# First attention of a macaron block: shared values weighed for two heads at once in three rounded passes, outputs one to two steps later

## What is computed

```python
q = (x @ w_q).reshape(bsz, q_len, 32, 128).transpose(0, 2, 1, 3)
k = (x @ w_k).reshape(bsz, q_len, 8, 128).transpose(0, 2, 1, 3)
v = (x @ w_v).reshape(bsz, q_len, 8, 128).transpose(0, 2, 1, 3)
lq = x @ w_lq
lk = (lq @ w_lk).reshape(bsz, q_len, 32, 128).transpose(0, 2, 1, 3)
lv = (x @ w_lv).reshape(bsz, q_len, 32, 128).transpose(0, 2, 1, 3)
...
k = jnp.repeat(k, 4, axis=1)
v = jnp.repeat(v, 4, axis=1)
attn = _causal_attn(q, k, v, SCALE)
lat = _causal_attn(q, lk, lv, SCALE)
...
return attn @ w_o + lat @ w_lo
```

## Time and profile before

| | us |
|---|---|
| median of 3 runs | 1806.8 |
| lowest, highest | 1804.63, 1810.41 |
| profiled execution, whole | 1806.92 |
| its span | 1805.0 |
| PE busy | 1739.7 (96%) |
| VectorE, ScalarE, GpSimd busy | 1098.4, 1084.0, 928.9 |
| granted clock of TensorE, mean | 0.997 of full |

### The profile page before, as it was taken

How to read it: one execution, slowest core, us unless ns; L and a number is a source line. 1 busy time by engine, 2 the same in 40 slices (tenths; PEclk the granted TensorE clock), 3 DMA queues, 4 the chain that set the end, 5 groups by cost and what they waited for, 6 DMA issues and landing times.

```text
span 1805.0 us, 32176 instructions
## 1 busy us (share of the span) xinstructions
PE 1739.7 (96%) x11116; PEld 1518.6 (84%) x11116; DVE 1098.4 (61%) x3305; ACT 1084.0 (60%) x3077; POOL 928.9 (51%) x1170
## 2 busy tenths in 40 slices
PE   7989999999999999999999999999999998899798
PEld 6779989989999998999999899989888776677567
DVE  6665465456456555644654664565565677888756
ACT  3355565566566656755665665576563264888964
POOL 4555544555554555554455555455542255777850
PEclk9999999999999999999999999999999999999999
DMA  4300021012001101200110120011012111000101
GB/s 145 108 22 13 7 71 36 1 36 71 7 17 61 36 1 42 65 7 19 59 36 1 48 65 1 18 60 36 1 54 64 42 52 55 1 2 2 37 12 47
DMA packets 35424, 65.79 MB, mean 36 GB/s; under 512 B 4032, under 2 KB 4672, under 8 KB 35264
## 3 DMA queue, kind: packets, MB, share of 16 engines
q1 hardware_dynamic: 35264, 63.73, 11.5%
HBM read 61.62 MB, written 2.10 MB: 35 GB/s over the span
## 4 chain that ended last, share of the span: by engine, by line
PE 74%; DVE 8%; ACT 8%; issue 6%; POOL 3%; DMA 0%; SPq 0%; DVEq 0%; POOLq 0%; ACTq 0%
PE bank L363 57%; PE bank L1105 6%; PE bank L1092 4%; PE bank L1107 3%; ACT s L1219 2%; PE bank L1677 2%; PE bank L1648 1%; ACT s L1743 1%; DVE h L761 1%; PE bank L1664 1%; DVE work L1324 1%; DVE work L772 1%; POOL h L839 1%; DVE x L1393 1%; ACT h L684 1%
## 5 line engine op out<-in xcount | busy, mean ns | idle before, releaser
L363 PE MATMUL bank<-W,oT 128*128 128x512 f32 x1632 | 432.1, 400 | 0.8 <-DVE x L1880 0.8
L1430 POOL TENSOR_TENSOR qk<-work,qk 128x512 fp32r<-128x512 f32 (+1 forms) x160 | 192.9, 1206 | 431.9 <-ACT qk L1210 431.8
L363 PEld LDWEIGHTS bank<-W,oT 128*128 128x128 f32 x1632 | 288.3, 189 | 48.5 <-DVE x L1880 1.2
L1226 ACT COPY pt<-bank 128x384 f32<-128x384 f32 x256 | 122.0, 476 | 324.1 <-PE bank L1092 323.8
L1422 POOL TENSOR_TENSOR work<-work,table 128x512 f32<-128x512 f32 (+1 forms) x160 | 191.3, 1195 | 134.3 <-ACT work L1205 134.3
L1219 ACT ACTIVATE s<-s,neg_max 128x128 f32<-128x128 f32 (+1 forms) x512 | 227.6, 445 | 49.8 <-DVE neg_max L1338 48.3
L363 PE MATMUL bank<-W,xnA 128*128 128x320 f32 (+1 forms) x1056 | 190.1, 334 | 2.3 <-DVE xnA L348 1.7
L1315 DVE TENSOR_TENSOR work<-bank,table 128x512 f32<-128x512 f32 (+1 forms) x160 | 102.0, 638 | 129.4 <-ACT work L1205 129.4
L363 PEld LDWEIGHTS bank<-W,xnA 128*128 128x128 f32 x1056 | 165.6, 188 | 14.7 <-DVE xnA L348 2.6
L363 PE MATMUL bank<-qk 128*128 128x256 f32 (+1 forms) x768 | 166.0, 351 | 0.9 <-POOL qk L1430 0.9
L1358 DVE COPY lvv<-bank 128x320 f32<-128x320 f32 x128 | 62.9, 491 | 170.1 <-PE bank L363 170.0
(11 more groups left out here) (111 smaller groups left out, 3495.9 us busy)
## 6 DMA issues: line engine op xcount, KB each, us to landing
raw<-in_weights SPq DMA_DIRECT2D x215, 256.0 KB, 2.7
x<-in_x SPq DMA_DIRECT2D x8, 256.0 KB, 5.2
out<-x SPq DMA_DIRECT2D x8, 256.0 KB, 2.1
row<-in_bias_rows SPq DMA_DIRECT2D x5, 256.0 KB, 2.8
table<-in_constants SPq DMA_DIRECT2D x4, 240.0 KB, 3.0
b_qk<-in_bias_rows SPq DMA_DIRECT2D x1, 512.0 KB, 3.7
b_val<-in_bias_rows SPq DMA_DIRECT2D x1, 256.0 KB, 3.1
table<-in_constants SPq DMA_DIRECT2D x1, 66.0 KB, 2.6
```

Of the source, the lines that this page charges most:

```text
L363: last = nc.tensor.matmul(out_ap, lhs(i), rhs(j), start=start and k == 0, stop=stop and k == 2)
L1226: nc.scalar.copy(pt0[:, k, :], bank[PT][:, 0:3 * P]).then_inc(a_pt, 1)
L1430: nc.gpsimd.tensor_tensor(lo, work[:, 2 + s, st.columns(what)], hi.bitcast(F32), ALU.subtract).then_inc(a_rope_lo, 1)
```

## The change

The shared values get a high and a low part of their own, `vs`. The shared probabilities of two heads are kept, in high and low parts, in `pt_pair`; the own probabilities stay in plain float32 (`pt_own`). In every second step (h=0 and h=2) `weigh_pair` multiplies both heads' shared probabilities by the shared values, in three passes of 512 columns and three of 256, and fills the whole bank `OB`. `weigh_own` is the weighing of before, for the own values alone, and stands once in each step. Results go to `o_pair` and `o_own`. The outputs of the shared part come one to two steps after the pair's weighing has its operands: none in h=2, two in h=1, one each in h=3 and h=0. Weight chunk 13 is split in step 3 instead of step 17, chunk 12 in 17 instead of 16, and the waits for chunks follow the new places of the outputs.

`turn(1)` now waits for `a_pt_lo`, the low part of the probabilities that `turn(0)` left in the bank. VectorE makes it (`turned_lo`) right behind the rotation.

```diff
-SPLIT_AT = {2: [17, 14], 3: [18], 11: [1], 12: [0, 2], 13: [3, 6], 14: [4, 7], 15: [8, 9],
-            16: [10, 11, 15, 12], 17: [16, 13]}
+SPLIT_AT = {2: [17, 14], 3: [18, 13], 11: [1], 12: [0, 2], 13: [3, 6], 14: [4, 7], 15: [8, 9],
+            16: [10, 11, 15], 17: [16, 12]}
...
-WEIGHTS_FOR = {2 + h: [C_WO + h, C_WLO + h] for h in range(GH)}
+WEIGHTS_FOR = {2: [C_WLO], 3: [C_WO, C_WLO + 1], 4: [C_WO + 1, C_WLO + 2],
+               5: [C_WO + 2, C_WO + 3, C_WLO + 3]}
...
-                lvv = sb(s, "lvv", [P, 2, LVW])
-                pt0 = sb(s, "pt0", [P, 2, 3 * P])
-                oT0 = [sb(s, f"oT0_{i}", [P, 4, SEQ], F32R) for i in (HI, LO)]
+                lvv = sb(s, "lvv", [P, 2, GH * HD])
+                vs = [sb(s, f"vs{i}", [P, 2, HD], F32R) for i in (HI, LO)]
+                pt_pair = [sb(s, f"pt_pair{i}", [P, 2, 3, P], F32R) for i in (HI, LO)]
+                pt_own = sb(s, "pt_own", [P, 3 * P])
+                o_pair = [sb(s, f"o_pair{i}", [P, 2, SEQ], F32R) for i in (HI, LO)]
+                o_own = [sb(s, f"o_own{i}", [P, 2, SEQ], F32R) for i in (HI, LO)]
...
             def turn(k):
-                n, s = st.near(-1).inst(k)
+                n, s = before.inst(k)
                 pe.wait_ge(a_norm, n + 1)
-                pe.wait_ge(a_pt, n + 1)
+                if k == 0:
+                    pe.wait_ge(a_pt_own, before.number() + 1)
+                else:
+                    pe.wait_ge(a_pt_lo, before.number() + 1)
                 for blk in range(3):
                     last = nc.tensor.transpose(bank[PT][:, blk * P:(blk + 1) * P],
                                                s0[:, s, blk * P:(blk + 1) * P], ident)
                 last.then_inc(a_turned, 1)
...
-            def weigh(k):
-                before = st.near(-1)
-                n, _ = before.inst(k)
-                col = before.h * P if k else GH * P
-                if before.h == 0 and k == 0:
+            def weigh_pair():
+                pe.wait_ge(a_pt_lo, before.number() + 1)
+                pe.wait_ge(a_own_lo, before.number() + 1)
+                to = bank[OB][:, :].rearrange("p (e q) -> p e q", e=2)
+                product(to, lambda p: vs[p][:, 0, :],
+                        lambda p: pt_pair[p][:, :, 0:2, :].rearrange("p e b q -> p e (b q)"), True, False)
+                product(to[:, :, P:SEQ], lambda p: vs[p][:, 1, :],
+                        lambda p: pt_pair[p][:, :, 2, :], False, True).then_inc(a_pv_pair, 1)
+
+            def weigh_own():
+                col = before.h * P
+                if before.h == 0:
                     pe.wait_ge(a_proj_free, before.fill(3)[0] + 3)
-                pe.wait_ge(a_pt, n + 2)
-                pe.wait_ge(a_o_lo, n + 1)
-
-                nc.tensor.matmul(bank[OB][:, 0:SEQ], lvv[:, 0, col:col + P], pt0[:, k, 0:2 * P],
+                pe.wait_ge(a_pt_own, before.number() + 2)
+                if before.paired():
+                    pe.wait_ge(a_pair_lo, before.pair() + 1)
+                else:
+                    pe.wait_ge(a_own_lo, before.number() + 1)
+
+                nc.tensor.matmul(bank[OB][:, 0:SEQ], lvv[:, 0, col:col + P], pt_own[:, 0:2 * P],
                                  start=True, stop=False)
-                nc.tensor.matmul(bank[OB][:, P:SEQ], lvv[:, 1, col:col + P], pt0[:, k, 2 * P:3 * P],
-                                 start=False, stop=True).then_inc(a_pv, 1)
-
-            def output(k):
-                done = st.near(-2)
-                n, s = done.inst(k)
-                first, end = done.h == 0 and k == 0, done.h == GH - 1 and k == 1
+                nc.tensor.matmul(bank[OB][:, P:SEQ], lvv[:, 1, col:col + P], pt_own[:, 2 * P:3 * P],
+                                 start=False, stop=True).then_inc(a_pv_own, 1)
...
+            def output(k, done):
...
+                if k:
+                    pe.wait_ge(a_own_lo, done.number() + 2)
+                    of, slot = o_own, done.number() % 2
+                else:
+                    pe.wait_ge(a_pair_lo, done.pair() + 1)
+                    of, slot = o_pair, done.h % 2
                 w = ((C_WLO if k else C_WO) + done.h) * CH
                 for tt in range(2):
-                    last = product(bank[OUTB[tt]][:, :], lambda p: oT0[p][:, s, tt * P:(tt + 1) * P],
+                    last = product(bank[OUTB[tt]][:, :], lambda p: of[p][:, slot, tt * P:(tt + 1) * P],
...
+            if lag2 and st.h == 0:
+                output(0, st.near(-3))
+            if lag1 and before.paired():
+                weigh_pair()
             if lag1:
-                weigh(0)
                 turn(1)
             if st.queries and not st.first:
                 a0_queries(pe, st)
@@ -1139,12 +1181,16 @@
                 if t == 0:
                     pe.wait_ge(a_proj_free, st.near(-1).fill("q")[0] + 3)
                 ln_turn(pe, 16 + t, t, t % 2, normed, banks=2)
-            if lag2:
-                output(0)
+            if lag2 and st.h in (1, 3):
+                output(0, st.near(-3))
+            if lag2 and st.h == 1:
+                output(0, st.near(-2))
+            if lag2 and st.h in (0, 2):
+                output(1, st.near(-2))
             if lag1:
-                weigh(1)
-            if lag2:
-                output(1)
+                weigh_own()
+            if lag2 and st.h in (1, 3):
+                output(1, st.near(-2))
...
+            def turned_hi():
+                act.wait_ge(a_turned, before.inst(0)[0] + 1)
+                nc.scalar.copy(pt_pair[HI][:, before.h % 2, :, :].rearrange("p b q -> p (b q)"),
+                               bank[PT][:, 0:3 * P]).then_inc(a_pt_hi, 1)
+
+            def turned_own():
+                act.wait_ge(a_turned, before.inst(1)[0] + 1)
+                nc.scalar.copy(pt_own[:, :], bank[PT][:, 0:3 * P]).then_inc(a_pt_own, 1)
...
+            def pair_hi():
+                act.wait_ge(a_pv_pair, before.pair() + 1)
+                nc.scalar.copy(o_pair[HI][:, :, :].rearrange("p e q -> p (e q)"),
+                               bank[OB][:, :]).then_inc(a_pair_hi, 1)
...
             if lagging(st):
-                turned_out(0)
+                turned_hi()
             if before.queries:
                 a0_rope_hi(act, before, "q")
...
+            if lagging(st) and before.paired():
+                pair_hi()
             if lagging(st):
-                result_hi(0)
-                turned_out(1)
+                turned_own()
...
-            def result_lo(k):
-                n, s = before.inst(k)
-                dve.wait_ge(a_o_hi, n + 1)
-                nc.vector.tensor_tensor(oT0[LO][:, s, :], bank[OB][:, 0:SEQ], oT0[HI][:, s, :].bitcast(F32),
-                                        ALU.subtract).then_inc(a_o_lo, 1)
+            def turned_lo():
+                dve.wait_ge(a_pt_hi, before.number() + 1)
+                hi, lo = [pt_pair[i][:, before.h % 2, :, :].rearrange("p b q -> p (b q)") for i in (HI, LO)]
+                nc.vector.tensor_tensor(lo, bank[PT][:, 0:3 * P], hi.bitcast(F32),
+                                        ALU.subtract).then_inc(a_pt_lo, 1)
+
+            def pair_lo():
+                dve.wait_ge(a_pair_hi, before.pair() + 1)
+                hi, lo = [o_pair[i][:, :, :].rearrange("p e q -> p (e q)") for i in (HI, LO)]
+                nc.vector.tensor_tensor(lo, bank[OB][:, :], hi.bitcast(F32),
+                                        ALU.subtract).then_inc(a_pair_lo, 1)
...
-                nc.vector.tensor_copy(lvv[:, tt, half * HALF:(half + 1) * HALF],
-                                      bank[fs][:, 0:HALF]).then_inc(a_proj_free, 1)
+                if half == 0:
+                    nc.vector.tensor_copy(lvv[:, tt, 0:HALF], bank[fs][:, 0:HALF]).then_inc(a_proj_free, 1)
+                    return
+                own = GH * HD - HALF
+                shared = bank[fs][:, own:HALF]
+                nc.vector.tensor_copy(vs[HI][:, tt, :], shared).then_inc(a_v_hi, 1)
+                nc.vector.tensor_copy(lvv[:, tt, HALF:GH * HD], bank[fs][:, 0:own])
+                dve.wait_ge(a_v_hi, st.values_before() + tt + 1)
+                nc.vector.tensor_tensor(vs[LO][:, tt, :], shared, vs[HI][:, tt, :].bitcast(F32),
+                                        ALU.subtract).then_inc(a_proj_free, 1)
 
             turn_of = None if st.last_group else st.g
             if before.queries:
                 a0_rotate(dve, before, "q")
+            if lagging(st):
+                turned_lo()
...
-            if lagging(st):
-                result_lo(0)
+            if lagging(st) and before.paired():
+                pair_lo()
...
             if lagging(st):
-                result_lo(1)
+                own_lo()
```

More of the change, by code:

```diff
@@ L901, in program @@
         a_turned = sem("a_turned")
[L902 to L905 removed]
+        a_v_hi = sem("a_v_hi")
+        a_pt_own = sem("a_pt_own")
+        a_pt_hi = sem("a_pt_hi")
+        a_pt_lo = sem("a_pt_lo")
+        a_pv_own = sem("a_pv_own")
```

(16 more changed lines are left out.)

26 lines of the change are left out of this document (12 added, 14 removed).

## The result

The changed kernel takes 1869.9 us (median of 4 runs, 1868.75 to 1870.97) against 1806.05 before: 1.0356 times as long, with a 95% interval of 1.0344 to 1.0368. The forecast was 1882, in a range from 1815 to 1905. It came out slower, as forecast, 12 us short of the number.

The account below looks back on a forecast made before the run. PE, busy 96% of the span, was taken as the bound, so its waits are lost time. 17 plain batches (26.9 us) and 15 split ones (48.0) add 74.9 to 1807, giving 1882 us; range 1815 to 1905.

Parts of the forecast that it names:

- PE works 0.24 less per pair: On PE, per pair of steps: two plain float32 weighings of 1.30 us become three passes costing 1.06; 15.4 us over 64 pairs.
- The low part takes 0.55: On VectorE, each step: making the low part of the shared probabilities, 384 columns, takes 0.55 us, between 0.42 and 0.69.
- h=1 waits 0.88: Step following the values: PE ready at 353.45, second turn possible at 354.33, so PE waits 0.88 us; step 1.62 longer.
- The handover: From VectorE's result to PE's effective start: 0.38 us, bounds 0 and 0.4.
- Plain h=3 waits 1.18: Second turn of h=3, unsplit chunks: PE waits 1.18 us for the low part; h=2 and h=3 together 0.45 shorter.
- Split batches 3.20 longer: 15 batches with two weight chunks split at h=2: 1.62 + 1.17 + 0.41 = 3.20 us longer each, 48.0 in all.
- that the gain comes through: First rival: PE finds every turn ready, time 1807 - 15 = 1791 us; chance 0.06.
- The bare handover: Second rival: the rotation is never late, each odd step waits 0.41 us, 1818 us in total; chance 0.10.
- the third, falling clock: Third rival: late turns delay following even steps, or TensorE's clock falls with waits, 1907 us; chance 0.12 shared with pair pass.
- The pair pass at 1.39: Fourth rival, on PE: the pair pass costs 1.39 us, 21 us more in total, 1903; held for part of the third, sharing 0.12.

## Why the prediction was right, and where it was off

- **PE works 0.24 less per pair**: right. The three passes took 1.05 by the distance of starts, 1.06 were forecast from the scores, and the plain pair 1.29. In plain batches the difference is 0.47 to 0.51 per batch. The strided output costs nothing extra. The rule of the Trainium skill (FP8 and Floating Point Precision, TensorE Precision Notes) that true FP32 takes four passes, which gave 20.5 us instead of 15.4, was further off than the row.
- **The low part takes 0.55**: right, 0.55.
- **h=1 waits 0.88**: 0.62 idle and 0.19 slower start, 0.81. The handover was taken as 0.38 from rows 8. Here it is 362.94 to 363.09 and 0.19, together 0.34.
- **Plain h=3 waits 1.18**: 0.98 + 0.19 = 1.17 in 6 of 15 batches, 1.13 + 0.19 = 1.32 in the other 9. The turn was late for the reason given, the sine product ahead of the rotation. A plain batch came out 1.50 longer than before, and 1.58 was forecast.
- **Split batches 3.20 longer**: this is the step that failed. They were 1.9 longer where the group's step 14 is the h=2, and 2.2 where step 2 is (medians). Measured was, in the same kind of batch as rows 7 and 8:

```profile
575.06 0.49 PE L1118 MATMUL bank<-table,s 128*128 128x128 f32 x3
...
576.47 0.69 DVE L1380 TENSOR_TENSOR work<-work 128x512 f32<-128x512 f32 x1
...
584.46 1.28 POOL L1500 TENSOR_TENSOR work<-work,table 128x512 f32<-128x512 f32 x1 [0.47 <-ACT work L1251]
...
587.08 0.52 PE L1118 MATMUL bank<-table,s 128*128 128x128 f32 x3 [2.06 <-DVE pt_pair L1407]
```

  The sum took the chain of the other engines as fixed to the start T of h=2 and added the new work to it. There it stood at T + 11.06 before (409.36 - 398.30), so T + 11.78 was forecast. It ended at 585.74, T + 10.68. The rotation of h=2, from which the chain runs on, started at T + 1.41. Before, it stood at T + 2.34:

```profile
400.64 0.69 DVE L1324 TENSOR_TENSOR work<-work 128x512 f32<-128x512 f32 x1
```

  So it was 0.93 earlier, where the forecast had it at its old place and the minima behind it 0.47 later. From the first queries of h=1 to T PE works 6.65 now (568.41 to 575.06), with three outputs, and worked 5.30 before (393.00 to 398.30), with two. VectorE's additions to x, which stand ahead of the rotation, began 0.44 before T, and 0.54 behind it before. The forecast added to the backlog of one step and did not take off what the longer step before it gave back.
- **The account of the profiled spans**, 1867.7 - 1805.0 = 62.7 against 74.9 forecast. From the second to the 30th batch the 15 plain ones became 22.2 longer together (forecast 23.7) and the 14 split ones 30.9 (44.8); of these 30.9 about 3.0 is a lower granted clock behind the waits of two batches. All the rest became 9.6 longer, against 6.4 for the three batches that the forecast had there: the last batch but one (from the values at 1336.48 to those at 1381.82) took 4.6 longer, and what follows it 4.2. So the split batches' term was too large by 17 us, and the falls of the clock and the end of the attention, which the sum left out, happened to give 6 of these back.
- **The rivals**: that the gain comes through fell by the result. The bare handover was refuted by putting the low part ahead of the rotation: 46 us went, and only then was it what PE waited for. Of the third, falling clock, a few us are in the changed kernel, and 28 in the one with the low part twice. The pair pass at 1.39 did not happen.

## What to carry to other kernels

A step inserted on a helper engine costs what its place in that engine's order makes it cost: ask what it stands behind, and what the bounding engine has left between the two things that it separates. With its 0.55 us behind the rotation and 1.06 us of cover, the kernel was 64 us slower. Ahead of it, and with an output between scores and turn, the kernel with the three passes came within 0.2% of the one before, and with the own weighing covered too it was 0.7% faster.

When a repaired version beats the old one by the expected number, run the repair without the original idea too: here the order alone gave 14 us to the plain format, and nothing was left of the 15 us expected of the rounded one. 8 of them came through once the weight splits were moved as well.

A run can also land on the expected time for another reason. Count the waits, by place and size, before calling the theory right: 17 waits of 1 us summed up like the 32 of 0.5 that were expected.

Chains of the other engines are not fixed to the start of the step in which they are read. If the step before gets longer, they catch up: here by 0.93 us.

## What the runs showed of the hardware

The granted clock of TensorE fell around some single waits of 2 to 3 us in an otherwise busy stretch. The changed kernel has nine waits of 2.0 to 2.5 us in the attention; at three of them the clock fell, and not at the two longest. At one of the three PE idled 2.06 us before a turn at 422.21, and the stretches read (columns as in the windows above):

```profile
415.00:420.00 5.00, 4.84 (x31) 3.89 (x29) 4.35 (x8) 4.92 (x14) 3.93 (x7) 1.00 0.09 12
420.00:425.00 5.00, 2.94 (x14) 2.82 (x14) 3.20 (x14) 3.26 (x12) 3.23 (x5) 0.71 0.35 98
```

That is 2.4 GHz, and then 1.2 GHz in part of the stretch. In the timeline of PE, the turn and the twelve 256-column products behind it, there and after the same wait in a later batch:

```profile
422.21 0.87 PE L1118 MATMUL bank<-table,s 128*128 128x128 f32 x3 [2.06 <-DVE pt_pair L1407]
422.74 2.91 PE L367 MATMUL bank<-xnA,W 128*128 128x256 f32 x12
...
587.36 1.67 PE L367 MATMUL bank<-xnA,W 128*128 128x256 f32 x12
```

The products took 2.91 in the one place and 1.67 in the other, where the clock stayed though the wait was 2.06 too; with the slower turn, 0.87 against 0.52, the fall cost about 1.6 us. The Trainium skill (TensorE: Matmul & The Clock Gate, What's actually happening) has the clock follow how busy TensorE was of late, as a monitor sees it that isn't aligned to the program, and these two places agree with that. So a wait on the bounding engine can cost more than its length: in the kernel with the low part twice, 28 us of slower work came with 34 us more of waits.
